# A state-space and mixture-of-experts layer on one core: arrivals in three stages, a pick in halves, batch 1's deviations on ScalarE and ten output buffers of their own

## The reference

```python
x = x + ga * mamba(h)
h = _layernorm(x) * (1 + cb) + sb
gate_logits = einsum('bsd,de->bse', h, gate_kernel)
top_k_weights, top_k_indices = lax.top_k(gate_logits, 2)
top_k_weights = softmax(top_k_weights)
h0, h1 = h @ w0_kernel[e], h @ w1_kernel[e]
x = x + gb * sum_over_picked_e(weight_e * (silu(h0) * h1) @ wo_kernel[e])
```

## Time and profile before

| | |
|---|---|
| median of 3 runs | 830.14 us (829.59 to 832.15) |
| the profiled execution, its own time | 826.15 us |
| its span, first to last instruction | 824.3 us |
| mean granted clock of PE | 0.963 of full |
| PE busy | 728.2 us, 88% |
| DVE, ACT, POOL busy | 623.2, 339.0, 512.5 us |

### The profile page before, as it was taken

The page is one execution under the profiler, slowest core; times in us unless marked ns, Lnnn a source line. Parts: engine busy times, 40 slices in busy tenths (PEclk is TensorE's granted clock), DMA queues, the critical chain, the costliest instruction groups (busy, mean ns, idle before and its releaser), DMA issues. The chain is left out here.

```text
span 824.3 us, 9267 instructions
## 1 busy us (share of the span) xinstructions
PE 728.2 (88%) x2233; PEld 361.5 (44%) x2234; DVE 623.2 (76%) x824; ACT 339.0 (41%) x383; POOL 512.5 (62%) x271
## 2 busy tenths in 40 slices
PE   5899998878787887878988988997899999999994
PEld 2444343323232332323534432466466656666662
DVE  4378889999999998999999998976454444454442
ACT  1777876445654544545545556421211111111110
POOL 1012234899999999999999998977533332322222
PEclk9999999999999999999999997997799999999998
DMA  9364644876768666677798989759553232223220
GB/s 289 96 169 146 198 162 113 204 196 161 208 159 210 167 166 188 170 195 179 201 237 215 250 204 251 208 138 336 174 150 58 46 47 40 47 39 49 37 30 1
DMA packets 62298, 126.43 MB, mean 153 GB/s; under 512 B 11898, under 2 KB 33850, under 8 KB 62140
## 3 DMA queue, kind: packets, MB, share of 16 engines
q1 hardware_dynamic: 50468, 116.12, 52.4%
q0 software_dynamic: 7152, 8.48, 6.0%
q10 hardware_dynamic: 4648, 1.48, 0.8%
HBM read 98.08 MB, written 24.69 MB: 149 GB/s over the span
## 5 line engine op out<-in xcount | busy, mean ns | idle before, releaser
L1710 POOL TENSOR_TENSOR pool<-pool,hT 128x1024 f32<-128x1024 f32 x92 | 214.6, 2355 | 11.8 <-PE PS L702 11.5
L1089 ACT ACTIVATE PS<-pool,negA 128x1024 f32<-128x1024 f32 x128 | 143.0, 1118 | 175.7 <-DVE pool L1400 175.6
L702 PE MATMUL PS<-pool,ident 128*128 128x512 f32 x368 | 187.2, 633 | 25.3 <-POOL pool L1710 24.6
L1795 POOL DMA_INDIRECT out<-uT,ptab x39 | 60.6, 1554 | 150.4 <-DVE uT L1635 114.7
L1400 DVE TENSOR_TENSOR_SCAN pool<-PS,pool 128x1024 f32<-128x1024 f32 x64 | 142.9, 2270 | 0.4 <-ACT PS L1089 0.4
L910 PE MATMUL PS<-pool,uT 128*128 (+1 forms) x312 | 142.3, 599 | 0.0
L702 PEld LDWEIGHTS PS<-pool,ident 128*128 128x128 f32 x368 | 68.0, 196 | 103.6 <-issue 51.7
L684 PE MATMUL PS<-pool 96*128 96x512 bf16 x256 | 79.2, 391 | 29.7 <-DVE pool L1388 14.6
L1605 DVE TENSOR_TENSOR uT<-uT,PS 128x512 f32<-128x512 f32 x39 | 26.8, 688 | 83.9 <-PE PS L910 81.0
L1710 POOL TENSOR_TENSOR Y<-pool,hT 128x1024 f32<-128x1024 f32 x36 | 84.0, 2358 | 3.3 <-PE PS L702 3.3
L1734 POOL TENSOR_TENSOR spread<-spread,pool 128x1024 f32<-128x1024 f32 x32 | 75.3, 2355 | 14.8 <-ACT spread L1095 14.7
(11 more groups left out here) (202 smaller groups left out, 870.8 us busy)
## 6 DMA issues: line engine op xcount, KB each, us to landing
hT<-C_scratch SPq DMA_DIRECT2D x128, 512.0 KB, 5.4
pool<-in_w SPq DMA_DIRECT2D x16, 512.0 KB, 7.9
uT<-expert_in_scratch SPq DMA_DIRECT2D x39, 130.5 KB, 2.1
Y<-Y SPq DMA_DIRECT2D x32, 128.0 KB, 2.4
C_scratch<-Y SPq DMA_DIRECT2D x8, 512.0 KB, 2.6
pool<-du_scratch SPq DMA_DIRECT2D x8, 512.0 KB, 7.9
Y<-in_wo SPq DMA_DIRECT2D x8, 512.0 KB, 7.9
expert_in_scratch<-zrow SPq DMA_DIRECT2D x16, 130.5 KB, 6.1
```

What stands on the lines that cost most here:

```text
L702: m = pe.matmul(PS[:, 6 + half, :], ident[:, :], prod_k[:, HF * half:HF * half + HF], start=False, stop=k == DS - 1)
L1089: act.activation(pair(2 * (k % 2)).unsqueeze(1), delta[:, chunk_at(g2, r), :], ACT.Exp, scale=decay[:, bass.ds(g2 * (2 * DS) + n, 1)]).the ...
L1710: gp.tensor_tensor(to, hst[:, k % HR, :], crep[k % RC], ALU.mult).then_inc(prod_done, 1)
L1795: gp.indirect_dma_start(out=out, out_offset=bass.IndirectOffsetOnAxis(ap=ptab[:, slot:slot + 1], axis=0), in_=yo[:, 2 + slot if slot < OWN ...
```

## The change

It has five parts.

1. **Three stages of arrival.** The sends of tiles 0 to 4 (the first ten) count on a semaphore of their own, `sent_early`. SP raises `arrived` to 1 when those ten have landed, POOL to 2 when all 16 of batch 0 have, and to 3 after batch 1's. `ranks(0)` gets five more small matmuls, which count the picks of tiles 0 to 4, and `place_of(0)` one more instruction: `ready` becomes 1, 2 or 3.
2. **Batch 1's deviations.** `rstd_of(2)` and `rstd_of(3)` leave POOL. DVE adds the epsilon at the end of `residual`, ACT takes the square root (`deviation`), and DVE takes the reciprocal between `centre` and `h2_of`.
3. **The pick in halves.** `best_of` (copy, `max`, `max_index`) runs for tiles 8 to 11 and for 12 to 15 apart. The logits of the two halves go to PSUM banks 6 and 7.
4. **Ten own output buffers** in place of six.
5. **Weights later.** `w0_of(4)`, `w0_of(5)` and the two stores stand behind the `rows_in` of experts 1 and 2, `w0_of(6)` behind that of expert 3, `w0_of(7)` and `w1_of(7)` behind that of expert 4.

```diff
-OWN_YO = 6
+OWN_YO = 10
+EARLY = 5
...
             sp.wait_ge(o_mm, NTB + 3)
             wo_of(3)
-            sp.wait_ge(o_mm, NTB + 5)
-            w0_of(4)
-            x2_stored(slice(NTB, NTB + TQ))
             sp.wait_ge(o_mm, NT)
-            w0_of(5)
-            x2_stored(slice(NTB + TQ, NT))
...
             sp.wait_ge(known, 1)
+            sp.wait_ge(sent_early, 16 * 2 * EARLY)
             sp.sem_inc(arrived, 1)
-            sp.wait_ge(sent[0], 16 * 2 * NTB)
...
                 rows_in(e * RT, e % 2)
+                if e == 1:
+                    w0_of(4)
+                    x2_stored(slice(NTB, NTB + TQ))
                 if e == 2:
+                    w0_of(5)
+                    x2_stored(slice(NTB + TQ, NT))
+                if e == 3:
                     w0_of(6)
-                if e == 3:
+                if e == 4:
                     w0_of(7)
-                if e == 4:
                     w1_of(7)
...
+                if not q:
+                    for j in range(EARLY):
+                        m = pe.matmul(PS[:, r_bank(q), at + NE:at + 2 * NE], ones[:, :], flat[:, NE * j:NE * j + NE],
+                                      start=j == 0, stop=j == EARLY - 1)
...
-            for t in range(NTB, NT):
-                take_h2(t)
+            def deviation(q):
+                tiles = slice(TQ * q, TQ * q + TQ)
+                act.wait_ge(rstd2_done, 4 + 3 * (q - 2) + 1)
+                act.activation(rstd[:, tiles], rstd[:, tiles], ACT.Sqrt).then_inc(rstd2_done, 1)
+
+            for q in (2, 3):
+                deviation(q)
+                for t in range(TQ * q, TQ * q + TQ):
+                    take_h2(t)
...
                 for t in range(first, end):
                     gathered(t)
+                dve.wait_ge(aggr2_done, end)
+                dve.tensor_scalar(rstd[:, first:end], mv[:, first:end, 1], EPS, None, ALU.add).then_inc(rstd2_done, 1)
...
                 for t in range(first, end):
                     centre(t)
+                dve.wait_ge(rstd2_done, 4 + 3 * (first // TQ - 2) + 2)
+                dve.reciprocal(rstd[:, first:end], rstd[:, first:end]).then_inc(rstd2_done, 1)
...
             residual(NTB + TQ, NT)
             normal_h2(NTB + TQ, NT)
+            best_of(1, NTB, NTB + TQ)
             pick(1)
...
-            send(0, slice(0, 6))
-            rstd_of(2)
-            send(0, slice(6, 11))
-            rstd_of(3)
-            send(0, slice(11, 16))
+            send(0, slice(0, 16))
+            gp.wait_ge(sent_early, 16 * 2 * EARLY)
+            gp.wait_ge(sent[0], 16 * 2 * (NTB - EARLY))
+            gp.sem_inc(arrived, 1)
             gp.wait_ge(ysum_done, RC + NG * DS)
             notes(1)
```

More of the change, by code:

```diff
@@ L270, in adaln_mamba_moe @@
         we_in = [sem(f"we_in{e}") for e in range(0, NE, 2)]
-        sent, xg_in = [sem(f"sent{q}") for q in range(NQ)], [sem("xg_in0"), sem("xg_in1")]
+        sent, sent_early, xg_in = [sem(f"sent{q}") for q in range(NQ)], sem("sent_early"), [sem("xg_in0"), sem("xg_in1")]
         xT_mm, xT_done, h0_mm, h01_mm, sil_done, inter_done = (sem(n) for n in ("xT_mm", "xT_done", "h0_mm", "h01_mm", "sil_done", "inter_done"))
@@ L296, in r_bank, with l_bank @@
             return 4 if q == 0 else 5 + q
+        def l_bank(t):
+            return 4 if t < NTB else 6 + (t - NTB) // TQ
         def delta_at(g):
@@ L515, in _ @@
                     sp.wait_ge(meta_done, 4 * (e - 1))
-                needed = sp.value_load(ready[0:1, e:e + 1], min_val=1, max_val=2)
+                needed = sp.value_load(ready[0:1, e:e + 1], min_val=1, max_val=3)
                 sp.wait_ge(arrived, needed)
                 rows_in(e * RT, e % 2)
+                if e == 1:
+                    w0_of(4)
+                    x2_stored(slice(NTB, NTB + TQ))
                 if e == 2:
+                    w0_of(5)
+                    x2_stored(slice(NTB + TQ, NT))
+                if e == 3:
                     w0_of(6)
-                if e == 3:
+                if e == 4:
                     w0_of(7)
-                if e == 4:
                     w1_of(7)
@@ L529, in _ @@
             sp.wait_ge(tails_out, 16 * NE)
-            sp.wait_ge(arrived, 2)
+            sp.wait_ge(arrived, 3)
             def row_of(slot):
@@ L867, in logits @@
                 for k in range(KD):
-                    m = pe.matmul(PS[:, 5 + q, NE * (t - GROUPS[q][0]):NE * (t - GROUPS[q][0]) + NE], h2s[:, t % 2, k, :], gate_sb[:, k, :],
+                    m = pe.matmul(PS[:, l_bank(t), NE * (t % TQ):NE * (t % TQ) + NE], h2s[:, t % 2, k, :], gate_sb[:, k, :],
                                   start=k == 0, stop=k == KD - 1)
@@ L1460, in h2_of @@
                 dve.wait_ge(centred, t - NTB + 1)
-                dve.wait_ge(rstd2_done, 2 * (t // TQ) + 2)
+                dve.wait_ge(rstd2_done, 4 + 3 * (t // TQ - 1))
                 if t == NTB:
@@ L1465, in h2_of, with best_of @@
                                          ALU.mult, ALU.add).then_inc(h2_rows, 1)
-            def pick(q):
-                first, end = GROUPS[q]
-                tiles, n = slice(first, end), end - first
+            def best_of(q, first, end):
                 if q:
                     dve.wait_ge(g_mm, end)
[L1472 to L1476, removed]
+                step(dve.tensor_copy(lgt[:, first:end, :].rearrange("p t n -> p (t n)"), PS[:, l_bank(first), 0:NE * (end - first)]))
                 settled()
@@ L1482, in pick @@
                     dve.max_index(i8[:, t, :], top8[:, t, :], lgt[:, t, :]).then_inc(index_done, 1)
+            def pick(q):
+                first, end = GROUPS[q]
+                tiles, n = slice(first, end), end - first
+                if q == 0:
+                    dve.wait_ge(lg0_done, 2)
+                    dve.wait_ge(scan_done, 2 + NG * DS)
+                    best_of(0, 0, NTB)
+                else:
+                    best_of(1, NTB + TQ, NT)
                 dve.tensor_tensor(w12[:, 0, tiles], top8[:, tiles, 1], top8[:, tiles, 0], ALU.subtract).then_inc(gap_done, 1)
@@ L1520, in place_of @@
                 if q == 0:
-                    step(dve.tensor_scalar(few, PS[:, r_bank(q), P + n * NE:P + n * NE + NE], float(P), 1.0, ALU.is_lt, ALU.add))
+                    counted = P + n * NE
+                    step(dve.tensor_scalar(few, PS[:, r_bank(q), counted + NE:counted + 2 * NE], float(P), 1.0, ALU.is_lt, ALU.add))
+                    settled()
+                    step(dve.scalar_tensor_tensor(few, PS[:, r_bank(q), counted:counted + NE], float(P), few, ALU.is_lt, ALU.add))
                     settled()
@@ L1657, in _ @@
             slots_of(1, between)
-            slots_of(2, None)
+            for s2 in range(2, OWN_YO // 2):
+                slots_of(s2, None)
             with dve.Fori(OWN_YO // 2, SPAIRS) as s2:
```

3 lines of the change are left out of this document (1 added, 2 removed).

## The result

The changed kernel takes 834.13 us (median of 20 runs) where the kernel before took 828.25 us on the same chip: a ratio of 1.0075, with an interval from 1.0058 to 1.0093. It is 6 us slower, where 3.8 us faster was forecast. A ratio compares executions of the two kernels and is not exactly the quotient of their medians; one execution of 967.48 us at a clock of 0.747, in the variant with rows of four, is left out of its ratio.

What follows compares the result with a forecast made beforehand. PE was taken as the bound before and behind its idle stretches and long slots. Terms 1.25 + 0.83 + 0.91 + 0.98 - 0.2 = 3.8 us came off the 830.14 us median, giving 826.3 us, range 823.6 to 829.4.

Steps and rivals of the forecast that it cites:

- Deviations by ScalarE and DVE: Before tile 12's transpose: DVE's 1.95 us wait for POOL's power goes, 0.70 us of add and reciprocal come in; gain 1.25 us.
- (e): Rival: slower, as the output adds start late behind batch 1's sends; gain gone at 6.6 us late, slower from 9.1; chance 0.06.
- The part on arrival: Before the first expert rows: ten sends 1.26 us apart let rows load early, so PE's wait of 0.91 us goes.
- ACT's square root shows nowhere: In batch 1's deviations: the root, about 0.21 us, is covered by DVE's centring of 1.66 us.
- 1.25 + 0.83 + 0.91: Gains in us between batch 1's projection and the first expert rows: deviations, pick in halves, arrival in stages.
- The half pick: Before the ranks: four tiles' max and max_index run ahead of the last logits, under PE's tiles 12 to 15; gain 0.83 us.
- The table load of 1.28 us ahead of the exponential: On ACT before pick(1)'s exponential: the load was to come some 1 to 2 us before its operand.
- the load ahead of the first silu: One of three ACT table loads; the trace was read as 1.28 us with no idle time behind it.
- Ten buffers: In the expert slots: leave no longer waits for yo_free, so two long slots return to 5.82 us; gain 0.98 us.
- Slot 12: First slot that could wait with ten buffers: its leave at 660.8 us, released at 660.5, so it doesn't wait.
- The clock: Open term, from tile 12 into the first slots: taken as unchanged, between 2.4 us more gained and 3.1 us lost.
- Rival (b): The clock stays up through tiles 12 to 15, 2.4 us more gained: 823.9 us; chance 0.11.

Runs made afterwards that it cites:

- rows of four: Changed kernel with three GpSimd pauses, each an add and power pair on constants, so sends stand in rows of four: 825.83 us, ratio 0.9972.
- Part 2 alone: Kernel before with the deviations moved to ACT and DVE as the only change, sixteen sends in one row: ratio 1.0106.
- first variant with dead pairs: Changed kernel with two unused add and power pairs on POOL, behind sends six and eleven: 824.01 us, ratio 0.9959; repeated, 823.49 us, ratio 0.9941.
- forty-eight memsets: Changed kernel with forty-eight small GpSimd memsets behind the sixth and again behind the eleventh send: 825.44 us, ratio 0.9979.

## Why the prediction was wrong, step by step

**The failed step is the one under "Deviations by ScalarE and DVE".** It counted the add, the root and the reciprocal that came in, and priced what went out only as "the wait of 1.95 us goes". The two power pairs were also the only pauses in POOL's sixteen sends, 2.85 and 2.71 us from send to send (558.09 to 560.94 and 566.40 to 569.11 in the kernel before) instead of 1.27. Without them signals of PE reach DVE, ACT and SP 3 to 11 us late. Part 2 alone makes the kernel 1.06% slower; two pauses that move the next send by 1.4 to 1.9 us, made of either kind of instruction, undo it. None of the rivals was this one: (e) had the right sign, by another mechanism, and its own 9 us of late adds are not what happened. The part on arrival used the same spacing of 1.26 us for all sixteen, so the unbroken row was written down, and taken for harmless. That two pauses of 1.4 to 1.9 us remove the loss and two of 0.34 us do not is shown; why a row holds signals back is not.

In detail, the 1.25 us of that step: in the first variant with dead pairs it is 3.8 us from the projection's end to the second `h2_of` (572.28 less 568.52), before 4.9 (569.01 less 564.1): a gain of 1.1 to 1.2 us. There ACT's root costs 0.17 us of waiting, as its copies come first in its order. In the stall the same order cost 3.61 us (583.52), since the root of the second half stands behind the four copies of the first. So "ACT's square root shows nowhere" holds only while the copies are in time.

**The rest of the stretch was right, given the pauses.** 1.25 + 0.83 + 0.91 of the sum lie between projection and first rows, 15.9 to 12.9 us; with the sends broken it measured 13.0 in both executions. The half pick gives 0.84 us (3.03 to 2.19 before the ranks) even in the slow kernel, and no wait for rows is left in either; in the variant with part 2 undone a late signal ate the 0.84 us. The table load of 1.28 us ahead of the exponential ended before its operand came: in the changed kernel it ran at 588.99, and the exponential at 591.34. So nothing came of what the Trainium skill (ScalarE: Activation LUTs, What ACT_TABLE_LOAD costs) says against mixing roots and exponentials: these traces agree on the load and show no cost for the switch. From the end of the last copy to the exponential it is 2.37 us with the load between (588.97 to 591.34), less than the 2.66 that the same section of the Trainium skill gives for load and drain, and 2.37 us in the variant with a copy for the root, which has no load there (581.98 to 584.35). The prediction read the load ahead of the first silu as having no idle time behind it; the trace has 1.73 us there, put down to PE, so that row could not tell. A copy in place of the root moved nothing.

**Ten buffers:** the size was right, the margin was not. Slot 12 was said not to wait by 0.3 us. It is held in 14 of the 16 profiles with ten buffers, by 0.92 to 5.03 us, and what that costs roughly follows the first add, as (e) said: where that comes 32.7 us behind the first `hidden` (615.91 less 583.21, first variant with dead pairs) the slot stays at 5.82 us; at 34.6 us (its repetition) the slot takes 7.41, at 34.0 (rows of four) 7.63, at 32.8 (the changed kernel) 6.60. Before, it was 29.3 us. So at the one end the whole 0.98 us is gained, and at the other the slot costs 1.6 to 1.8 us, more than the two that it replaced. In these four the adds start 3.4 to 5.3 us later than before. Part 5 has a share in that: with it undone the first add came at 30.6 us. In the changed kernel:

```profile
676.95 0.38 PE L902 MATMUL PS<-ident,uT 128*128 128x128 f32 x2
683.55 0.38 PE L902 MATMUL PS<-ident,uT 128*128 128x128 f32 x2
```

```profile
680.50 0.48 DVE L1661 SCALAR_TENSOR_TENSOR uT<-PS,wtab,uT 128x256 f32<-128x256 f32 x1 [3.99 <-POOLq L1820]
```

**The sum** of 3.8 us stands against what the two dead pairs measured, 0.41% and 0.59%, that is 3.4 and 4.9 us. The forecast described that kernel, not the one it was made for, and that its number fits there is in part luck: 2.9 us are seen up to the first rows, but from there to the end of the span it is 244.3 us before and 242.5 and 244.8 in the two profiles, which shows no 0.98 us.

**The clock** did as the forecast took it, nearly: the first slot's eight matmuls took 5.42 us before, 5.78 in the changed kernel, 5.09 and 5.07 with dead pairs, and 4.73 to 6.18 in the other fifteen profiles. Rival (b) came true once, in part: with forty-eight memsets, after 1.38 us of idle time, the granted clock was still 1.00 from 567.4 to 569.4 us, where tile 12 is turned (its transposes took 0.44 us, not 0.69), and 0.53 from there to 572.5.

**What stays open** is why a row of sends holds back PE's signals. PE ran on up to its next wait, DVE's own steps followed each other without a gap, and the sends went on at their pace. It could be the number of sends in flight or what POOL writes for each; no run here tells them apart. Full transfer engines alone are not it: their busy share is 1.07 from 560 to 570 us before, with signals on time, and 1.05 from 564 to 574 in the changed kernel. The profile models the ends of matmuls, so a result that is written late cannot be told from a signal that is late; PE's next matmuls beginning on time speaks for the signal, but is no proof. The kernel breaks batch 1's sixteen sends by itself into 6, 5 and 5, with a wait for landing between; batch 0's had the same 6, 5 and 5 by the power pairs.

## What to carry to other kernels

An instruction that is taken out of a row on another engine is an edit of that row, even where nobody waits for it: ask what its time kept apart. When an engine waits and the one it waits for is long done, look at what a third engine does then, and undo the parts one by one before explaining; here one part explained all, and two short pauses turned a loss of 0.75 to 1.0% into a gain of 0.4 to 0.6%. Give `yo`-like buffers a margin of several microseconds, not 0.3, where their release hangs on a series of transfers.

## What the runs showed of the hardware

- With GpSimd's indirect sends of 128 rows in one row, 1.27 us apart, and other transfers in flight, TensorE's semaphore signals to VectorE, ScalarE and SyncE came 3 to 11 us late from about the seventh or eighth send of the row on. They came one after the other. In the changed kernel the last was used 0.7 us after the last send's end (580.35 and 581.00), in its repetition 2.3 us (577.43 and 579.68), in part 2 alone 2.5 us (572.24 and 574.78).
- In rows of four and five sends single signals still came 1.0 to 1.7 us late (with part 2 undone, with forty-eight memsets, with rows of four).
- Two pauses that moved the next send by 1.4 to 1.9 us took the long delays away; by 0.34 us they did not, nor did 0.05 us after every send.
- A row of memsets of one column on GpSimd goes at 0.035 us each (0.49 us for fourteen, 1.70 for forty-eight), though a single one of 4 or 8 columns is shown with 0.11 to 0.13 us.
